# Scores and values of the local attention on row tiles of 64 rows, their mask from ScalarE, layer norm on ScalarE, new orders of work

## Time and profile before

| | |
|---|---|
| median of 3 runs | 1965.3 us (1964.91 to 1966.18) |
| the profiled execution | 1965.16 us, its span 1963.4 us |
| PE busy | 1874.6 us (95%) |
| PEld busy | 1510.2 us (77%) |
| DVE busy | 1643.9 us (84%) |
| ACT busy | 1390.9 us (71%) |
| POOL busy | 1378.3 us (70%) |
| DMA | 70.32 MB, mean 36 GB/s |

### The profile page before, as it was taken

The page is one execution under the profiler, slowest core; times in us unless marked ns, Lnnn a source line. Parts: engine busy times, 40 slices in busy tenths (PEclk is TensorE's granted clock), DMA queues, the critical chain, the costliest instruction groups (busy, mean ns, idle before and its releaser), DMA issues. The chain is left out here.

```text
span 1963.4 us, 54531 instructions
## 1 busy us (share of the span) xinstructions
PE 1874.6 (95%) x21027; PEld 1510.2 (77%) x21027; DVE 1643.9 (84%) x3362; ACT 1390.9 (71%) x2676; POOL 1378.3 (70%) x1394
## 2 busy tenths in 40 slices
PE   7999868999999999999999999999999999999996
PEld 5888747778777877887787788778778877877874
DVE  5887757898898888889888988988898898889873
ACT  4777736776777677777767777777777677677762
POOL 4777757776877677777768767777776687676661
PEclk8999989999999999999999999999999999999998
DMA  4000011110111111110101211011111101110100
GB/s 133 2 1 2 1 45 42 34 36 21 52 45 49 31 30 30 55 50 23 49 21 30 65 33 50 21 39 56 44 28 40 30 21 39 32 51 20 38 22 22
DMA packets 46293, 70.32 MB, mean 36 GB/s; under 512 B 15567, under 2 KB 29781, under 8 KB 46037
## 3 DMA queue, kind: packets, MB, share of 16 engines
q1 hardware_dynamic: 44564, 64.73, 11.3%
q10 hardware_dynamic: 1472, 2.10, 0.3%
HBM read 21.72 MB, written 1.05 MB: 12 GB/s over the span
## 5 line engine op out<-in xcount | busy, mean ns | idle before, releaser
L1094 POOL TENSOR_TENSOR ra<-ra,rb 128x512 f32<-128x512 f32 x384 | 487.6, 1282 | 70.1 <-DVE rb L1090 68.3
L1132 POOL TENSOR_TENSOR qn<-ra,rs 128x512 f32<-128x512 f32 x384 | 394.2, 1049 | 53.7 <-DVE rs L1125 53.7
L1206 POOL TENSOR_TENSOR pr<-pr,rl 128x512 f32<-128x512 f32 x192 | 200.4, 1044 | 268.2 <-DVE rl L1200 268.2
L1069 DVE TENSOR_REDUCE ss<-sq 128x8 f32<-128x512 f32 x384 | 259.5, 676 | 16.8 <-ACT sq L1058 11.6
L1196 DVE TENSOR_REDUCE sm<-pr 128x8 f32<-128x512 f32 x192 | 130.4, 679 | 13.9 <-ACT pr L1192 13.9
L1192 ACT ACTIVATE pr<-dif 128x512 f32<-128x512 f32 x192 | 121.5, 633 | 21.9 <-PE pT L1212 13.8
L1222 ACT COPY pt<-pT 64x512 f32<-64x512 f32 x144 | 83.0, 577 | 64.8 <-PE pT L1212 64.0
L1337 DVE TENSOR_SCALAR early<-fx,fmv,frs 128x128 f32<-128x128 f32 x96 | 69.5, 783 | 43.0 <-POOL frs L322 43.0
L1240 PE MATMUL pS<-pt,vs 128*64 128x64 f32 x1536 | 101.8, 229 | 0.4 <-ACT pt L1222 0.4
L1240 PEld LDWEIGHTS pS<-pt,vs 128*64 128x64 f32 x1536 | 77.4, 137 | 29.5 <-issue 28.5
L492 POOL TENSOR_TENSOR ra<-ra,rb 128x512 f32<-128x512 f32 x64 | 81.5, 1291 | 24.9 <-DVE rb L488 24.9
(11 more groups left out here) (346 smaller groups left out, 6224.6 us busy)
## 6 DMA issues: line engine op xcount, KB each, us to landing
vs<-v SPq DMA_DIRECT2D x96, 384.0 KB, 3.3
wqkvA<-in_L_ffn_Wqkv SPq DMA_DIRECT2D x18, 512.0 KB, 5.0
vs<-v SPq DMA_DIRECT2D x96, 64.0 KB, 3.0
woB<-in_L_ffn_Wo SPq DMA_DIRECT2D x6, 512.0 KB, 4.0
w<-in_L_ffn_W SPq DMA_DIRECT2D x6, 341.0 KB, 2.9
out<-x SPq DMA_DIRECT2D x4, 256.0 KB, 2.3
x<-in_L_attn_x SPq DMA_DIRECT2D x1, 768.0 KB, 8.2
w<-in_L_ffn_W SPq DMA_DIRECT2D x12, 64.0 KB
```

The costliest lines, as they stand in the source:

```text
L1069: e.tensor_reduce(ss[:, j, :], sq[:, j % 2, :].rearrange("p (h d) -> p h d", d=DB), AX.X, ALU.add).then_inc(b_ss.sem, 1)
L1094: e.tensor_tensor(ra[:, j, :], ra[:, j, :], rb[:, j % 2, :], ALU.add).then_inc(b_ad.sem, 1)
L1132: e.tensor_tensor(qn[:, j % 4, :].rearrange("p (h d) -> p h d", d=DB), ra[:, j, :].rearrange("p (h d) -> p h d", d=DB), rs[:, c % 2, 8 * j ...
L1206: e.tensor_tensor(y, y, rl[:, s, :].unsqueeze(2).to_broadcast([P, 8, 64]), ALU.mult).then_inc(b_pn.sem, 1)
```

## The change

In words; "a unit" of scores is 128 partitions by 512 columns, one bank, as before.

- **scores** has two calls a batch instead of four. Each has 64 matmuls: 64 rows of input (one head), 32 columns of weights (a window's queries), 64 streamed (keys). The two heads of a pair lie in partitions 0 to 63 and 64 to 127 and write to two different banks. q is copied whole to a new `qT`; `qd`, its zeros and their memset go.
- **The mask** is written to the bank by ScalarE (`mask`, four a batch, each behind a wait for its bank). Ahead of the stream TensorE writes the six banks once more (`mark_written`).
- **values** has two sets of four calls a batch, each call 16 matmuls: 64 rows, 64 columns of weights, 32 streamed; the two row halves write to two banks. `copy_p` and `turn_copy` are one instruction each. `copy_o` writes to `oT` with a stride.
- **Softmax buffers**: `dif` and `pr` (two units each) become `sp` with four units, overwritten in place; `less_max` waits for `turn_p` of the unit in the batch before.
- **Norm steps**: the chain has 12 steps without scalar_tensor_tensor. Steps 0 and 1 stay on VectorE, 2 to 11 go to GpSimd.
- **Layer norm** is four ScalarE activations with a scale and a bias; GpSimd computes the bias in two more steps in `l_root`.
- **The bias b2** is an 86th row of `w2` for the last chunk, with a row of ones in `gT`; `l_bias`, `b2b` go.
- **xt_turn** reads `xr`; `xt_copy` goes.
- `turn`, `turn_p`, `l_turn` use `flip`, the same transpose, with `start` on the first of four only.
- SyncE: `load_hidden` and `load_second` come before `move_values(2, 1)`; the bias load joins `w2`'s.
- All bank tables and the four lists of the pair are new.

```diff
-NORM = 9
+NORM = 12
@@ xt_turn
-            e.wait_ge(b_xc.sem, b_xc.at(it))
+            e.wait_ge(f_x.sem, f_x.at(l * FP + c // 2 - FP))
+            xc = xr[:, (c % B) * NT:(c % B + 1) * NT, :]
@@ norm_step
-            elif n in (2, 6):
-                e.scalar_tensor_tensor(t, y, 1.0, x_, ALU.mult, ALU.mult).then_inc(b_rs.sem, 1)
-            elif n in (3, 7):
-                e.scalar_tensor_tensor(t, t, 1.0 if n == 3 else -1.0, y, ALU.mult, ALU.mult).then_inc(b_rs.sem, 1)
+            elif n in (2, 8):
+                e.tensor_tensor(t, y, x_, ALU.mult).then_inc(b_rs.sem, 1)
+            elif n in (3, 9):
+                e.tensor_tensor(t, t, y, ALU.mult).then_inc(b_rs.sem, 1)
             elif n == 4:
-                e.scalar_tensor_tensor(t, t, -10.0 / 3.0, t, ALU.add, ALU.mult).then_inc(b_rs.sem, 1)
+                e.tensor_scalar(p, t, -10.0 / 3.0, None, ALU.add).then_inc(b_rs.sem, 1)
...
@@ turn_copy
+            dst = kT[g][:, :, WIN + t * P:WIN + (t + 1) * P] if isk else qT[g][:, :, t * P:(t + 1) * P]
+            e.copy(dst, w.rearrange("p (h q) -> p h q", h=4)).then_inc(b_tc.sem, 1)
+        def mark_written(e):
+            for n in SCORE_BANKS:
+                e.matmul(banks[n], ident16[:, :], maskB[:, :], start=True, stop=True)
+        def mask(e, l, c, u):
+            e.copy(banks[SCORE_BANK[c % 2][u]], maskB[:, :]).then_inc(b_mk.sem, 1)
@@ scores
-            o = banks[SCORE_BANK[c % 2][u]]
-            e.matmul(o, ident16[:, :], maskB[:, :], start=True, stop=False, skip_group_check=True)
...
+            o = [banks[SCORE_BANK[c % 2][2 * g + h]] for h in range(2)]
+            e.wait_ge(b_mk.sem, b_mk.at(it, 2 * g + 1))
+            for k in range(4):
+                for a in range(2):
+                    lo = (2 * k + a) * 2 * WIN
+                    for j in range(4):
+                        w = 4 * (j // 2) + 2 * a + j % 2
+                        for h in range(2):
+                            r = slice(64 * h, 64 * h + 64)
+                            i = e.matmul(o[h][WIN * j:WIN * j + WIN, lo:lo + 2 * WIN],
+                                         qT[g][r, k, WIN * w:WIN * w + WIN],
+                                         kT[g][r, k, WIN * w:WIN * w + 2 * WIN],
+                                         start=False, stop=True, skip_group_check=True)
@@ values
+            o = [banks[VALUE_BANK[c % 2][2 * g + a]] for a in range(2)]
+            for j in range(4):
+                lo = k * P + j * WIN
+                for h in range(2):
+                    f = k * P + 64 * h
+                    for a in range(2):
+                        r = slice(64 * a, 64 * a + 64)
+                        i = e.matmul(o[a][64 * h:64 * h + 64, lo:lo + WIN], (v if j % 2 else vs)[g][r, j // 2, f:f + 64],
+                                     pt[r, g, h, lo:lo + WIN], start=(k == 0 and j == 0), stop=True,
+                                     skip_group_check=True)
@@ l_root
+            e.tensor_tensor(fnb[:, :], fmv[:, :, 0], frs[:, :], ALU.mult).then_inc(f_rs.sem, 1)
+            e.wait_ge(f_rs.sem, f_rs.at(it, 2))
+            e.tensor_scalar(fnb[:, :], fnb[:, :], -1.0, None, ALU.mult).then_inc(f_rs.sem, 1)
@@ l_norm
-                i = e.tensor_scalar(fln[:, t, :], fx[:, t, :], fmv[:, t, 0:1], frs[:, t:t + 1],
-                                    ALU.subtract, ALU.mult)
+                i = e.activation(fln[:, t, :], fx[:, t, :], ACT.Identity, bias=fnb[:, t:t + 1], scale=frs[:, t:t + 1])
```

More of the change, by code:

```diff
@@ L1140, in turn @@
             for p in range(4):
-                i = e.transpose(o[:, p * P:(p + 1) * P], qn[:, j % 4, p * P:(p + 1) * P], ident)
+                i = flip(e, o, p, qn[:, j % 4, p * P:(p + 1) * P])
             i.then_inc(b_tr.sem, 1)
@@ L1220, in copy_p @@
[L1220 to L1231 removed]
+            e.wait_ge(b_pv.sem, b_pv.at(it - 1, 4 * g + 3))
@@ L1236, in values @@
-            for t in range(NT):
-                for par in range(2):
-                    for h in range(2):
-                        lo = pair * P + 64 * h
-                        i = e.matmul(o[64 * h:64 * h + 64, t, :, par, :], (v if par else vs)[g][:, t, lo:lo + 64],
-                                     pt[:, u % 2, 2 * p2 + t, par, :, WIN * h:WIN * h + WIN],
-                                     start=(p2 == 0 and t == 0 and par == 0), stop=True, skip_group_check=True)
+            o = [banks[VALUE_BANK[c % 2][2 * g + a]] for a in range(2)]
@@ L1356, in l_turn @@
             for t in range(FT):
-                i = e.transpose(o[:, t * P:(t + 1) * P], fln[:, t, :], ident)
+                i = flip(e, o, t, fln[:, t, :])
             i.then_inc(f_lt.sem, 1)
@@ new lines, in pair_dve @@
+            if on(p) and last(p):
+                scaled_rope(e, l + 1)
+            if on(p - 1):
+                out_add(e, l, c - 1)
+            if on(p):
+                row_max(e, l, c, 2)
+                less_max(e, l, c, 2)
+                row_max(e, l, c, 3)
+                less_max(e, l, c, 3)
+                row_sum(e, l, c, 2)
+                row_inverse(e, l, c, 2)
+            if on(p - 1):
+                l_stats(e, l, p - 1)
+            if on(p):
+                row_sum(e, l, c, 3)
+                row_inverse(e, l, c, 3)
@@ new lines, in pair_dve, with pair_pool @@
+            if on(p - 1):
+                l_moments(e, l, p - 1)
+            if on(p):
+                row_max(e, l, c + 1, 0)
+                less_max(e, l, c + 1, 0)
+                row_max(e, l, c + 1, 1)
+                less_max(e, l, c + 1, 1)
+        def pair_pool(e, l, p, on):
+            c = 2 * p
+            if on(p - 1):
+                normalise(e, l, c - 1, 4)
+            if on(p - 1) and last(p - 1):
+                split_low(e, l + (p - 1) // FP + 1, 1, 2)
+            if on(p - 1):
+                rotate_add(e, l, c - 1, 6)
+                rotate_add(e, l, c - 1, 7)
+                normalise(e, l, c - 1, 5)
+                normalise(e, l, c - 1, 6)
+                soft_norm(e, l, c - 1, 0)
+            if on(p):
+                rotate_add(e, l, c, 0)
+                rotate_add(e, l, c, 1)
+                rotate_add(e, l, c, 2)
+            if on(p - 1):
+                soft_norm(e, l, c - 1, 1)
+                normalise(e, l, c - 1, 7)
+            if on(p):
+                rotate_add(e, l, c, 3)
+                rotate_add(e, l, c, 4)
+                rotate_add(e, l, c, 5)
+                rotate_add(e, l, c, 6)
@@ L1953, in pair_pool @@
+                rotate_add(e, l, c, 7)
+                norm_step(e, l, c, 10)
+                norm_step(e, l, c, 11)
+                normalise(e, l, c, 0)
+                normalise(e, l, c, 1)
+                normalise(e, l, c, 2)
+            if on(p) and last(p):
+                split_low(e, l + 1, 0, 0)
+            if on(p):
+                normalise(e, l, c, 3)
             if on(p - 1):
                 soft_norm(e, l, c - 1, 2)
-            if on(p - 2):
-                l_bias(e, l, p - 2)
+            if on(p):
+                rotate_add(e, l, c + 1, 0)
```

894 lines of the change are left out of this document (401 added, 493 removed).

## The result

The changed kernel takes 2058.9 us (median of four runs, 2043.3 to 2064.4) against 1965.3 before (1964.9 to 1966.2): ratio 1.046, 95% interval 1.040 to 1.052. The forecast was 1814. So 94 us were lost where 151 were expected to be won. The profiled execution has a span of 2062.6 us.

What follows compares the result with a forecast made beforehand. TensorE's instruction stream was taken as the bound, 67.9 us a pair. Gains of 125 us in 19 pairs, 20 in five weight-split pairs, and 3 each at start and tail, off 1965.2, gave 1814 us (8 in 10: 1740 to 1900).

Steps and rivals of the forecast that it cites:

- Old tile work: TensorE's scores and values before the change, with switches between whole array and parts: 22.4 us a pair.
- Scores, 4.8 us a pair: New scores on TensorE: four calls a pair of 128 records, eight array parts overlapping, 1.2 us each (0.9 to 1.8).
- Values, 7.4 us and bound by weight loads: New values on TensorE: four sets a pair at 1.86 us, limited by loading 64 weight columns, so no gain.
- TensorE at 59.7 us a pair: TensorE's work per pair of batches: 67.8 less 22.4 of old tile work plus 14.3 of new.
- GpSimd's step, 0.40 us: Each norm step moved to GpSimd takes 0.40 us (0.31 to 0.51), twenty a pair, 8.0 us.
- GpSimd bound (the second case): Rival: slower norm steps put GpSimd at 56.7 us, making a pair 64.4 us; 1893 us in all, chance 0.17.
- Masks hidden on ScalarE: ScalarE's eight mask writes a pair, 4.6 us, cost nothing thanks to its slack; 1 us a pair if uncovered.
- Wait allowance, 1.6 us a pair: Added to TensorE's 59.7 us for waits on GpSimd (54.5) and VectorE (53.1), making a pair 61.3 us.
- The clock stays full: TensorE's granted clock: a lower level in mid-stream was listed as a sign of being wrong, without size or chance.
- The start and the tail, 3 us each: Savings outside the pairs: 3 us at the start, where zeroing qd goes, and 3 after the last pair.
- The slower case: Rival: row halves don't overlap (2013 us), or each matmul has a floor of time (about 2090); chance 0.09.
- PE gets shorter and nothing comes of it: Rival: waits take all of TensorE's gain, requiring every engine's load wrong by 6 us; 1965 us, chance 0.02.

Runs made afterwards that it cites:

- e7: Changed kernel with the mask written by TensorE again (a matmul ahead of each bank's scores) instead of by ScalarE; 2058.3 us.
- e15: Kernel before the change, with the third product of each projection (low part of x by high part of weights) left out; 1899.4 us.
- e1: Changed kernel with TensorE test blocks of scores-shaped, values-shaped and mixed matmuls put in ahead of the stream, results thrown away; ran once, no total time given.
- e8: Changed kernel with out_proj moved between values and scores in a pair's first half, and the next pair's xt_turn between last scores and last values; 2062.6 us.
- e2: Changed kernel with matmuls of out_proj, proj and xt_turn put in between those of four of the eight dense scores and values runs; 2194.6 us.
- e3: Changed kernel with zero-weight full-array matmuls of 512 columns added within scores and values, nothing moved; 2245.4 us.
- e4: Changed kernel with 3082 small TensorE semaphore instructions, placed so that few 256-instruction block ends lie behind dense runs; 2257.9 us.
- e5: Changed kernel with 3000 small TensorE semaphore instructions, placed so that many 256-instruction block ends lie behind or in dense runs; 2427.5 us.

## Why the prediction was wrong, step by step

- **Old tile work, 22.4 us a pair.** Right; it is from rows.
- **Scores, 4.8 us a pair (0.9 to 1.8 a call).** 1.41 us a call where no bracket is in it, 5.7 a pair. Row halves do overlap; the spacing was 11 ns where 9.4 was taken.
- **Values, 7.4 us and bound by weight loads.** 0.467 us for 32 records, 1.87 a set: right to 1%.
- **TensorE at 59.7 us a pair.** 61.25 in a pair at full clock, 61.7 by the fit. The saving was some 6 to 6.8 us a pair of the 8.1 forecast. The mean middle pair is 72.6 us where 61.3 was forecast: 61.7 of work, 3.3 for the clock and 7.6 idle.
- **GpSimd's step, 0.40 us.** 0.406 from start to start. GpSimd's 54.5 us a pair: 54.6 on average. GpSimd bound (the second case): not seen; TensorE waited 4 us for it in all. ScalarE has 46.8 us a pair and VectorE 52.8, as reckoned (46.8 and 53.1). These loads were right.
- **Masks hidden on ScalarE.** Right by e7.
- **Wait allowance, 1.6 us a pair.** This is the step that failed. It is 212 / 24 = 8.8. About 4.7 are block ends, a cost for which neither the sum nor a rival had a place, though the kernel before showed the fetches; 4.1 are waits for the other engines, of the kind that e15 brings out in the kernel before, at 62.6 us of TensorE's work in a pair of 65. The allowance was set from loads (54.5 against 59.7), and loads don't tell the length of a chain.
- **The clock stays full.** The text named a lower clock in mid-stream as what would make it wrong, and gave it no chance and no price. It costs 94 us at most, about 72 by the fit. It comes mostly behind idle time of TensorE, which it makes dearer; which kind of idle time brings it is open.
- **The start and the tail, 3 us each.** Neither came. The stream's first projection begins at 277.69 us instead of 277.10, because the six matmuls that write the banks stand ahead of it, and from the last pair's start to the end it is 135.6 us instead of 131.1, longer by about what a pair is.
- **Rivals.** The slower case (row halves or a floor of time for each matmul, 2013 or 2090) gave the right side for a wrong reason: e1 and the stream have neither. "PE gets shorter and nothing comes of it" (1965, at 0.02) is nearest in mechanism, but it had waits take the gain with the loads wrong by 6 us; the other engines' loads were right, and waits and clock took more than the gain. No case had that.

What stays open: how the idle time and the time would shrink if only the block ends went. The runs that removed them changed the order or added instructions as well, and in the one that added nothing (e8) the idle time at block ends was halved and waits took its place. Open too is which of this brings the clock down: e2 lost half of the block-end brackets and kept its 231 us at the lower level, e3 and e7, which added full-array matmuls, had 39 and 145.

## What to carry to other kernels

Price a matmul by its instructions too: where 256 TensorE instructions in a row took 1.4 or 1.9 us, the fetch of the next block was often late, here by 1.4 us on average, and alone such a run takes 3.5 to 3.7 us. From what length on the fetch is covered no run shows. Cutting one engine's work pays only as far as the next chain, and a run that leaves some of that work out shows how far this is before the tiles are rewritten. Idle brackets on TensorE can be paid twice, once as they are and once by the clock behind them.

## What the runs showed of the hardware

- A fetch of 16 KB takes 0.9 to 1.5 us on its queue, and where a bracket stands matmuls go on 2.2 to 3.0 us after its start.
- A dense run alone: 3.5 to 3.7 us for 256 instructions, whether the matmuls need 1.4 or 1.9.
- Matmuls on quarters of the array keep the 2.4 GHz level if nothing interrupts them (e1, 21 us); at the end of a bracket of 4.8 us the level fell to 1.2 GHz, and with five brackets of 1.2 to 1.7 us in 20 us it stayed up until the last matmul; the 3.4 us behind that were at 1.2 GHz.
- A full-array matmul between matmuls of parts costs about 0.2 us beyond its own columns.
- A semaphore increment of its own on TensorE costs 0.05 to 0.07 us where several stand in a row (149 us for 3082 in e4, 206 for 3000 in e5).
